# Routing one-hots from bf16 operands, expert owners on GpSimd, an early spare gather, and a new order for the low parts, in a Perceiver block on one core

## What is computed

```python
x = x + xattn(layernorm(x), ctx_1024, ...)   # 4 x 4096 keys of width 256, one head, then w2 on [x, output]
x = x + local_attn(layernorm(x), ...)        # 16 heads, window 64
x = x + moe(layernorm(x), gate_w, wg, wu, wd)
# moe, on 1024 rows of 256, 8 experts of inner width 1024:
logits = x_flat @ gate_w.T
top_v, top_i = top_k(logits, 2); probs = softmax(top_v)
out = sum over experts e of combine[e] * ((silu(x_flat @ wg[e].T) * (x_flat @ wu[e].T)) @ wd[e].T)
```

## Time and profile before

| | |
|---|---|
| median of three runs | 635.04 us (634.96 to 638.15) |
| the profiled execution's own time | 635.36 us |
| its span | 633.6 us |
| mean granted TensorE clock | 0.982 |
| TensorE matmul busy | 598.0 us, 94% of the span |
| VectorE busy | 457.9 us, 72% |
| ScalarE busy | 336.0 us, 53% |
| GpSimd busy | 255.7 us, 40% |
| DMA | 152.62 MB, mean 241 GB/s |

### The profile page before, as it was taken

How to read it: one execution, slowest core, us unless ns; L and a number is a source line. 1 busy time by engine, 2 the same in 40 slices (tenths; PEclk the granted TensorE clock), 3 DMA queues, 4 the chain that set the end, 5 groups by cost and what they waited for, 6 DMA issues and landing times. The chain is left out here.

```text
span 633.6 us, 10820 instructions
## 1 busy us (share of the span) xinstructions
PE 598.0 (94%) x4008; PEld 514.0 (81%) x4008; DVE 457.9 (72%) x803; ACT 336.0 (53%) x603; POOL 255.7 (40%) x313
## 2 busy tenths in 40 slices
PE   8999999899999999999999858999999999999993
PEld 7889988898889988996667646788888888888882
DVE  4867588767886697769888957776767767677750
ACT  4447522762367334554776652656565655657540
POOL 3317820784058433684454613123132332323312
PEclk9999999999999999999999977999999999999998
DMA  8988887899869647861000346999999999999933
GB/s 286 321 305 234 259 324 207 224 278 315 279 190 281 196 134 183 235 172 43 1 3 1 135 141 233 377 333 336 350 323 360 325 343 339 340 353 335 358 100 83
DMA packets 66035, 152.62 MB, mean 241 GB/s; under 512 B 7504, under 2 KB 47952, under 8 KB 55088
## 3 DMA queue, kind: packets, MB, share of 16 engines
q1 hardware_dynamic: 61568, 145.91, 68.8%
q0 software_dynamic: 4416, 6.03, 5.5%
HBM read 121.52 MB, written 31.46 MB: 241 GB/s over the span
## 5 line engine op out<-in xcount | busy, mean ns | idle before, releaser
L630 ACT ACTIVATE wide_high<-region_a 128x1024 fp32r<-128x1024 f32 (+1 forms) x108 | 105.6, 994 | 101.5 <-PE psum L1599 89.6
L1078 DVE TENSOR_TENSOR wide_low<-region_a,wide_high 128x1024 fp32r<-128x1024 f32 x92 | 112.2, 1221 | 64.0 <-ACT wide_high L630 64.0
L566 POOL TENSOR_TENSOR wide_low<-region_a,wide_high 128x512 fp32r<-128x512 f32 x64 | 82.4, 1290 | 18.4 <-ACT wide_high L630 14.4
L1616 PE MATMUL psum<-region_a,region_w 128*128 128x256 f32 x368 | 83.2, 379 | 0.3 <-ACT region_w L630 0.3
L1379 PE MATMUL psum<-turned_high,wide_low 128*128 128x256 f32 x256 | 79.6, 311 | 2.4 <-DVE turned_low L989 1.5
L1599 PE MATMUL psum<-wide_high,turned_low 128*128 128x512 f32 x184 | 77.9, 424 | 1.5 <-issue 0.8
L1616 PEld LDWEIGHTS psum<-region_a,region_w 128*128 128x128 f32 x368 | 69.6, 190 | 10.7 <-issue 0.5
L1379 PE MATMUL psum<-turned_high,wide_high 128*128 128x256 f32 x256 | 72.4, 283 | 0.0
L1379 PE MATMUL psum<-turned_low,wide_high 128*128 128x256 f32 x256 | 72.2, 282 | 0.0
L1599 PE MATMUL psum<-wide_high,turned_high 128*128 128x512 f32 x184 | 72.1, 392 | 0.0
L1599 PE MATMUL psum<-wide_low,turned_high 128*128 128x512 f32 x184 | 71.9, 391 | 0.0
(11 more groups left out here) (201 smaller groups left out, 1205.4 us busy)
## 6 DMA issues: line engine op xcount, KB each, us to landing
region_a<-turned_up SPq DMA_DIRECT2D x23, 2048.0 KB, 9.9
region_a<-turned_down SPq DMA_DIRECT2D x23, 1024.0 KB, 7.5
region_a<-ctx_dram SPq DMA_DIRECT2D x16, 1024.0 KB, 8.9
turned_up<-region_w SPq DMA_DIRECT2D x64, 256.0 KB, 4.2
region_w<-L_ffn_wg_dram SPq DMA_DIRECT2D x16, 512.0 KB, 6.4
region_w<-L_ffn_wu_dram SPq DMA_DIRECT2D x16, 512.0 KB, 6.1
region_w<-L_ffn_wd_dram SPq DMA_DIRECT2D x16, 512.0 KB, 5.8
turned_down<-region_w SPq DMA_DIRECT2D x32, 256.0 KB, 4.2
```

What stands on the lines that cost most here:

```text
L566: nc.gpsimd.tensor_tensor(val_lo[:, g % 4], ctx_sb[n][:, g * PAIR:(g + 1) * PAIR, :], val_hi[:, g % 4].bitcast(F32), ALU.subtract).then_in ...
L630: return nc.scalar.activation(dst, src, ACT.Copy)
L1078: nc.vector.tensor_tensor(w_lo[:, k % RING], group_of(k), w_hi[:, k % RING].bitcast(F32), ALU.subtract).then_inc(low_ready, 1)
L1616: last = nc.tensor.matmul(bank[6][:, 0:D], hidT[n][:, ic * P:(ic + 1) * P], rows, start=ic == 0, stop=ic == IC - 1)
```

## The change

- **Layout and types.** `place_row`, `place_tile`, `place_prob`, `is_tile`, `ways` have the pick as the innermost index now, and `is_tile`, `ways` and the two columns compared (`row_b`, `tile_b`) are bf16. The one-hots compare with full bf16 tables `each_row` and `each_tile` in place of short rows that were broadcast. TensorE reads one pick of them, so with a step of 16 elements (32 bytes).
- **Tables.** GpSimd writes the two tables by `iota` (2048 and 368 columns) into the end of `region_w`, behind its last layer norm work. `row_numbers` and `tileno` go.
- **`tile_i`** (a shift) goes; `tile_b` is slot minus row, so 128 times the tile, and waits for `row_i`.
- **Owners.** `begun` and `owner` leave VectorE. GpSimd computes them on one partition, in seven instructions, each waiting for the one before.
- **Spare gather.** Once the rows and the zeros are stored, GpSimd gathers 128 spare rows into `xg[3]`, ahead of `owners()`; the gathers of the tiles wait for it, and for the tokens.
- **Order of parts.** In each group `xgT_hi*w_lo`, `xgT_hi*w_hi`, then `xgT_lo*w_hi`. Group 0 waits for the high part of the rows, and only its third matmul for the low part.
- **Tile 1's rows.** At j = 0 VectorE splits tile 1's rows ahead of `low(4)` rather than behind it.

```diff
-        place_row = place_row_f.bitcast(BF16).rearrange("p (i r) -> p i r", i=PICKS)
+        place_row = place_row_f.bitcast(BF16).rearrange("p (r i) -> p r i", i=PICKS)
...
+        _, each_tile_f, each_row_f = cut(region_w, [4 * MAT - PICKS * (SLOT_TILES + P) // 2, PICKS * SLOT_TILES // 2, PICKS * P // 2])
...
-        place_tile = place_tile_f.bitcast(BF16).rearrange("p (i v j) -> p i v j", i=PICKS, v=2)
+        place_tile = place_tile_f.bitcast(BF16).rearrange("p (v j i) -> p v j i", i=PICKS, v=2)
...
+            pool.wait_ge(w_stored[1], 16 * QUADS * E * NMAT // 2 + FIRST)
+            nc.gpsimd.iota(each_row, pattern=[[1, P], [0, PICKS]], base=0, channel_multiplier=0,
+                           allow_small_or_imprecise_dtypes=True).then_inc(tables_ready, 1)
+            nc.gpsimd.iota(each_tile, pattern=[[P, SLOT_TILES], [0, PICKS]], base=0, channel_multiplier=0,
+                           allow_small_or_imprecise_dtypes=True).then_inc(tables_ready, 1)
+
+            def owners():
+                pool.wait_ge(first_found, 1)
+                nc.gpsimd.tensor_tensor(begun, tile_start[0:1, :].rearrange("p (a j) -> p a j", a=1).broadcast_to([1, E - 1, SLOT_TILES]),
+                                        first[0:1, 1:E].rearrange("p (e a) -> p e a", a=1).broadcast_to([1, E - 1, SLOT_TILES]),
+                                        ALU.subtract).then_inc(owner_step, 1)
+                pool.wait_ge(owner_step, 1)
+                nc.gpsimd.tensor_scalar(begun, begun, 1.0 / P, 1.0, ALU.mult, ALU.add).then_inc(owner_step, 1)
+                pool.wait_ge(owner_step, 2)
+                nc.gpsimd.tensor_scalar(begun, begun, 0.0, 1.0, ALU.max, ALU.min).then_inc(owner_step, 1)
+                pool.wait_ge(owner_step, 3)
+                nc.gpsimd.tensor_tensor(begun[:, 0:3], begun[:, 0:3], begun[:, 3:6], ALU.add).then_inc(owner_step, 1)
...
+                nc.gpsimd.tensor_copy(owner[0:1, :], begun[:, 0]).then_inc(owner_ready, 1)
...
             pool.wait_ge(rows_stored, 16 * DUOS)
             pool.wait_ge(zero_stored, 16)
+            pool.wait_ge(w_turned, E * NMAT * STEPS)
+            pool.indirect_dma_start(out=xg[AHEAD - 1], out_offset=None, in_=x3_dram,
+                                    in_offset=bass.IndirectOffsetOnAxis(ap=spare_i[:, 0:1], axis=0)).then_inc(spare_gathered, 16)
+            owners()
+            pool.wait_ge(spare_gathered, 16)
             pool.wait_ge(tokens_ready, 1)
...
-            then(nc.vector.tensor_reduce(first[:, :], started, axis=X_AXIS, op=ALU.add))
-            then(nc.vector.tensor_tensor(begun, tile_start[:, :].rearrange("p (j a) -> p j a", a=1).broadcast_to([P, SLOT_TILES, E - 1]),
-                                         first[:, 1:E].rearrange("p (a e) -> p a e", a=1).broadcast_to([P, SLOT_TILES, E - 1]), ALU.is_ge))
-            with nc.allow_low_precision(reason="a count up to 7"):
-                nc.vector.tensor_reduce(owner[:, :], begun, axis=X_AXIS, op=ALU.add).then_inc(owner_ready, 1)
+            nc.vector.tensor_reduce(first[:, :], started, axis=X_AXIS, op=ALU.add).then_inc(first_found, 1)
+            dve.wait_ge(first_found, 1)
...
-            nc.vector.tensor_scalar(row_i[:, :], slot[:, :], P - 1, None, ALU.bitwise_and)
-            then(nc.vector.tensor_scalar(tile_i[:, :], slot[:, :], P.bit_length() - 1, None, ALU.logical_shift_right))
+            then(nc.vector.tensor_scalar(row_i[:, :], slot[:, :], P - 1, None, ALU.bitwise_and))
+            nc.vector.tensor_tensor(tile_b[:, :], slot[:, :], row_i[:, :], ALU.subtract)
+            nc.vector.tensor_copy(row_b[:, :], row_i[:, :])
+            then(nc.vector.tensor_tensor(ways[:, 0, :], way_base[:, :], row_i[:, :], ALU.subtract))
...
+            dve.wait_ge(tables_ready, 2)
+            then(nc.vector.tensor_tensor(is_tile, each_tile, per_pick(tile_b[:, :], SLOT_TILES), ALU.is_equal))
             for v in range(2):
-                nc.vector.tensor_tensor(place_tile[:, :, v, :], is_tile, ways[:, :, v:v + 1].broadcast_to([P, PICKS, SLOT_TILES]), ALU.mult)
+                nc.vector.tensor_tensor(place_tile[:, v], is_tile, per_pick(ways[:, v], SLOT_TILES), ALU.mult)
             for n in range(TOPK):
                 half = slice(n * TILES, (n + 1) * TILES)
-                nc.vector.tensor_tensor(place_row[:, half, :], row_numbers[:, :].rearrange("p (a r) -> p a r", a=1).broadcast_to([P, TILES, P]),
-                                        per_pick(row_i[:, half], P), ALU.is_equal).then_inc(places_ready, 1)
+                nc.vector.tensor_tensor(place_row[:, :, half], each_row[:, :, half], per_pick(row_b[:, half], P), ALU.is_equal).then_inc(places_ready, 1)
...
-                last = nc.vector.tensor_tensor(place_prob[:, :, v, :], is_tile, per_pick(prob_parts[:, v], SLOT_TILES), ALU.mult)
+                last = nc.vector.tensor_tensor(place_prob[:, v], is_tile, per_pick(prob_parts[:, v], SLOT_TILES), ALU.mult)
...
-                if j + 1 < SLOT_TILES:
+                if j == 0:
+                    tile_xgT(1, 1)
+                    low(4)
+                elif j + 1 < SLOT_TILES:
                     low(4 * j + 4)
                     tile_xgT(j + 1, 1 - n)
...
-                    last = nc.tensor.matmul(bank[6][:, 0:2 * SLOT_TILES], place_row[:, i, :], place_tile[:, i].rearrange("p v j -> p (v j)"),
+                    last = nc.tensor.matmul(bank[6][:, 0:2 * SLOT_TILES], place_row[:, :, i], place_tile.rearrange("p v j i -> p (v j) i")[:, :, i],
                                             start=i == 0, stop=i == PICKS - 1)
...
-                        pe.wait_ge(xgT_ready, j + 1)
+                        pe.wait_ge(xgT_high, j + 1)
...
-                        parts = ((xgT_lo, w_hi), (xgT_hi, w_lo), (xgT_hi, w_hi))
+                        parts = ((xgT_hi, w_lo), (xgT_hi, w_hi), (xgT_lo, w_hi))
                         for m, (rows, w) in enumerate(parts):
+                            if g == 0 and c == 0 and m == 2:
+                                pe.wait_ge(xgT_ready, j + 1)
```

39 lines of the change are left out of this document (21 added, 18 removed).

## The result

| | before | after |
|---|---|---|
| runs on the same chip, median | 635.4 us (7 runs) | 639.57 us (7 runs, 638.87 to 641.29) |
| ratio, 95% interval | | 1.0065 [1.005, 1.008] |
| profiled execution | 635.36 us | 639.5 us |
| its span | 633.6 us | 637.8 us |
| mean granted clock | 0.982 | 0.978 |

The change makes the kernel 4.1 us slower. The forecast was 632.9 us, with nothing slower than 636.3 in its range. The two spans differ by 4.2 us, so the pair of profiles can be read for it.

The account below looks back on a forecast made before the run. TensorE bounds the expert loop, and VectorE's routing chain, then TensorE's own order, time its start. Terms -2.03 + 0.75 - 0.45 - 0.45 = -2.18 us took 635.36 to 633.2, forecast as a 632.9 median; range 631.0 to 636.3.

Parts of the forecast that it names:

- Owners on GpSimd: In the routing, GpSimd's seven owner instructions take 4.0 us; tile 1's load goes out later but still in time for ScalarE.
- cover of gather 0: Ahead of tile 0's transposes: gather 0 takes 3.3 to 4.9 us and stays hidden, at worst 0.4 us showing.
- The tables go where GpSimd idles: Before the tokens: GpSimd writes the tables (2416 columns) in its 17.69 us of idle time; no cost was counted.
- Rival 4: TensorE's chain in the routing: the clock comes back sooner, change -3.6 us, time 631.4; chance 0.14.
- rival 2: In the routing, GpSimd's seven owner instructions stretch beside VectorE's work, leaving a gain of 0.8 us, 634.2; chance 0.14.
- Stepped reads: TensorE's inverse and weights matmuls read with a 32-byte step: +0.75 us, between free and a bound of 1.5.
- Rival 1: TensorE's stepped pairs cost more than a load's own length; at 0.16 us a pair other gains are eaten; chance 0.12.
- One-hots from bf16: VectorE's one-hot comparisons in the routing run at twice the rate with 2-byte operands: -1.63 us.
- Owners leave VectorE, and one more wait: VectorE's routing chain: two owner instructions gone, -0.60 us; one added wait for `row_i`, +0.20.
- Spare gather: On GpSimd ahead of gather 0: may shorten the 0.92 us between tokens and gather 0; credited 0.
- Low part last: Start of tile 0: its matmuls begin when the rows' high part is done, not the low part, -0.45 us.
- Tile 1's rows sooner: Start of tile 1: rows split ahead of `low(4)` let it start sooner, net -0.45 us.

Follow-up runs that it names:

- e9: Kernel before, with only the owners moved to GpSimd: ratio 1.0068, 638.17 us.
- e1: Changed kernel, with the two tables written earlier, during local attention (the large one in four pieces): ratio 1.001, 636.97 us.
- e2: Changed kernel, with the owners back on VectorE and the tables still late: ratio 0.9996, 635.62 us.
- e6: e1, with tile 1's load issued only once gather 0 has landed: ratio 1.0043.
- e15: The same kernel as e1, run again in more rounds: ratio 1.0023, 638.06 us.
- e10: Changed kernel, with two more filling matmuls ahead of tile 0's transposes: ratio 1.0031, 637.47 us.
- e4: Kernel before, with the 2048-column table written by GpSimd in the changed kernel's place and never read: ratio 0.9992, 635.08 us.
- e13: e8, with three filling matmuls ahead of the weights instead of four and none behind: ratio 0.9971, 633.96 us.
- e12: e8, with the weights' 16 matmuls moved behind tile 0's up matmuls: ratio 0.9985, 633.2 us.
- e7: e1, without the spare gather: ratio 1.0016.
- e5: Kernel before, with only the loop order changed (low part last, tile 1's rows ahead of low(4)): ratio 0.9991, 635.58 us.
- e8: Changed kernel, with both tables early and owners back on VectorE: ratio 0.998, 635.61 us.
- e11: e8, with the weights' 16 matmuls reading neighbouring columns instead of every 16th: ratio 0.9979, 633.66 us.
- e3: Kernel before, with one-hots stored pick-innermost but still computed from f32 and int32: ratio 1.0186.
- e14: e9, with five filling matmuls instead of one ahead of tile 0's transposes: ratio 1.0039, 637.61 us.
- e16: e8, with two filling matmuls ahead of the weights instead of four and none behind: ratio 0.9979, 634.66 us.

## Why the prediction was wrong

**Owners on GpSimd: the step that failed is the cover of gather 0, "at worst 0.4 shows".** The owners' length was right: 3.57 us, forecast 4.0. That the load would go out later was right, and that the gather would be issued into it was in the text. What was mis-sized is what that does to the gather. I put it at 3.3 to 4.9 us, the upper end from gather 2, which flew beside SyncE's store, so that at worst 0.4 us would show; 1.22 showed in the kernel after and 3.04 in e9. The gather measured 5.9 (after), 6.0 (e1) and 6.3 (e9), and in each of the three it lands within 0.4 us of the load: 391.4 and 391.5, 390.4 and 390.6, 389.5 and 389.9. Where the load landed ahead of it (e2: 387.8 and 388.1) or was issued behind it (e6), the gather took 2.8. The 0.5 us between that and the 3.3 of the kernel before is GpSimd's own instruction, 0.95 us in e2 and 1.49 before: the landing is 1.8 to 1.9 us behind its end in both. The row that I took as the bound had shown as much already. The view of DMA issues, before, has for the store, issued at 388.19:

```profile
sums_by_token<-residual SPq DMA_DIRECT2D x1, 1024.0 KB, 4.8
```

It landed at 393.0, and gather 2, issued at 388.42, at 393.3. I carried over the length of that gather, and not that it lands with the transfer ahead of it; by my own figures the load was to land at 389.7, 2.3 us behind the transposes' 387.4. I had asked only whether the load comes in time for ScalarE.

**The idle TensorE costs a second time, and no step had that.** Rival 4 asked whether the clock would come back sooner; it did, in the window from 387.50, in place of 388.5. The same row showed nothing of what a pause behind it does. In the kernel after it fell 0.8 us into a pause of 1.2, and tile 0's first matmuls ran at about 0.43 us apart: this ate the 0.8 us that tile 1 gained (+0.03 in the table). In e1's profile a pause of 1.75 us left the clock up; in that of e15, the same kernel, it fell in a pause of 1.25. So it is a chance that a pause brings, and the filled versions price it at 1 to 2 us. Nor is the sooner return shown to be the change's: e10 has the same instructions up to the fillers behind the weights, and its clock came back at 392.25.

**"The tables go where GpSimd idles": right for GpSimd, wrong for VectorE.** GpSimd did idle there, but VectorE ran the norm beside it, and its instruction became 2.35 us long. It ended 0.14 us behind the second table (369.32 + 0.54), in e4 0.15 behind the first. The Trainium skill (SBUF — State Buffer, "Who interferes with whom") says that VectorE's `tensor_scalar` in a two-port mode and GpSimd block each other for a whole instruction; these two rows agree, the second table's 0.54 us included. I had applied the rule to the owners (rival 2) and not to the tables. What it costs is less settled. Alone nothing (e4, 0.9992). Undone in the changed kernel, e15 gives 0.4% back and e1 0.5%. One part of the first maximum's lateness is the clock: it fell at 370.5 in the kernel after, ahead of the last 16 logits matmuls, and at 371.5 before, in the middle of them; they took 3.42 us for 2.32. This fall moves by itself: from the norm to the first maximum the four profiles with a late table show 5.5 to 6.9 us and all others 3.5 to 6.5, and e4's has 5.53 without a loss in its time. A cost of 0.2% would fit both e4's interval and the difference between the kernel after and e15; whether the table costs more in company than alone stays open.

**Stepped reads: right direction, too small.** From the end of `place_row` to the end of the inverse it is 1.12 us, before 0.55 (+0.57); the weights +1.16. That is 1.7, forecast 0.75, bound 1.5. The bound was "each pair takes as long as its weight load, 0.117". The inverse stayed inside its part of it (0.79), the weights went beyond theirs (0.73). The 0.117 was read from the inverse alone; the weights' matmuls had longer loads already in the kernel before. Views of line 1562 before and of line 1582, the inverse, after (shortest, median, longest ns):

```profile
L1562 PEld LDWEIGHTS psum<-region_s x16: 133/138/151, 386.4 to 387.6; 128*128 128x128 bf16 x16
```

```profile
L1582 PEld LDWEIGHTS psum<-region_s x16: 142/149/170, 382.5 to 383.8; 128*128 128x128 bf16 x16
```

Nor does a pair follow its load: in the kernel after, the loads of inverse and weights are equally long (median 0.149 and 0.148), but a pair of the inverse, with 46 moving columns, takes 0.104 us and one of the weights, with 69, 0.144. That points to the moving operand, at an estimated 0.040 / 23 = 1.7 ns a column from these two figures; no run varied it alone. Rival 1 asked for this, and its break-even, 0.16 us a pair, was not reached. The note on 16-byte lines in the Trainium skill (SBUF — State Buffer, "Door 1: The DMA port swizzle") agrees in direction: a step of 32 bytes goes to a new line each time. The doubling that I weighed is what 1.14 (before) and 2.29 (e13) show at 1.2 GHz; at 2.4 GHz it is threefold, 0.71 (e9) to 2.31 (e12).

**One-hots from bf16: right.** -1.50, forecast -1.63. A `place_row` takes 0.702 us; before, the two took 2.35. The view of line 1178, shortest, median and longest ns:

```profile
L1178 DVE TENSOR_TENSOR region_s<-region_w,row_of_pick x2: 682/702/722, 381.7 to 382.3; 128x1024 bf16<-128x1024 bf16 x2
```

The Trainium skill (VectorE: DVE Perf Modes, "The perf-mode tier table") has twice the rate for this, and for the part of the time that goes by columns the trace now agrees.

**Owners leave VectorE, and one more wait: -0.17, forecast -0.40.** From `first_tile` to `is_tile` it is 2.02 us, before 2.19. Beside GpSimd's steps VectorE's own became slower, `row_i` 0.28 for 0.17 and the two of `picked` 0.47 for 0.36; in e2, without those steps, they are back at 0.17 and 0.36. That is rival 2's contention, with the other engine paying.

**Spare gather: 0, as forecast.** No gain can be seen in e7 either.

**Low part last: right.** In e2, at full clock, transposes to first matmul are 0.46 us shorter, forecast 0.45.

**Tile 1's rows sooner: right to tile 1, wrong to the end.** Tile 1 gained 0.8 in e5, forecast 0.45. But it does not come off the end. Tile 2's up load is issued only when a buffer of tile 0's is read, and ScalarE waits for it 2.24 us in the kernel after and 2.29 in e5, 1.25 before. Over both tiles e5 gains nothing (-0.80 + 1.02). "Each microsecond by which the loop starts earlier should come off the end" does hold, as far as tile 2, for the start of tile 0: from its first matmul to tile 2's first silu it is 19.9 to 20.1 us in e1, e2, e5, e8, e10 and e11, whose tile 0 starts 16.1 to 18.9 us behind the first maximum (before: 17.44, and 19.82 from there). e2 and e8 come out only even because they start tile 0 only 1.04 and 0.67 us sooner, not the 2 us and more of the forecast, and lose 0.2 of it by tile 2 (0.84 and 0.46).

**Later in the loop,** the +0.81 us is one late load at tile 13. The profiles of e3, e6, e10, e12, e14 and e15 have 0.3 to 0.9 us there too, those of e11, e13 and e16 at other tiles, and those of the kernel before, e1, e2, e4, e5, e7, e8 and e9 at most 0.25 at any. As e1 and e15 are the same kernel and e3 and e14 have little of the change in them, it moves from execution to execution and is not the change's.

**In sum.** The forecast's -2.18 and the span's +4.2 are 6.4 us apart. By the stretches of the first table: 1.85 lie ahead of the routing's first maximum, where I had nothing; 0.6 up to the tokens (-1.12, forecast about -1.7), half of it the stepped reads of the inverse; 1.9 up to tile 0's first matmul (+1.88, forecast about 0), of which 0.8 lies ahead of the wait (some 0.7 of it the weights' stepped reads, by e11), 1.2 is the wait for gather 0, and behind it 0.15 is gained, the low part's 0.46 less 0.3 for the lowered clock; 0.5 at tile 1 (the gain eaten by the lowered clock); 1.0 at tile 2's load; 0.8 at tile 13; and -0.2 at the end. These were read from one pair of profiles, whose stretches move by a microsecond or two from run to run. What the ratios show is shorter: with the owners on VectorE the loss is gone (e2), and with the owners on GpSimd alone it is all there (e9). One slip of the prediction changes nothing: its upper end, 636.3, is a rival 1 with pairs of 0.20 us; 0.21 would give 636.6.

## What to carry to other kernels

When a step is moved to a slower engine, follow what it releases to the end: here the result was not late for anyone, but the load that it released now flew together with a gather that the critical chain needs, and the gather landed when the load did. Take from a row when a transfer landed beside another, not only how long it took. Work put where its own engine idles can still hold up a neighbour, as the tables did VectorE. And a pause of TensorE just behind the return of its clock may have to be paid twice: take it away, or else fill it.

## What the runs showed that I had not expected

- A gather issued 1.5 to 2 us behind a 2 MB load lands with the load (5.9 to 6.3 us), and in 2.8 us when the load lands ahead of that (e2) or is issued later (e6).
- TensorE's pairs of 69 columns that read both operands with a step of 32 bytes take 0.144 us at 1.2 and at 2.4 GHz; plain ones take 0.071 and 0.044. Pairs of 46 columns take 0.104 with the step and 0.061 without, at 1.2 GHz.
- VectorE writing 2-byte results with a step of 32 bytes took 4.6 us for 1024 columns (e3), and 1.2 with neighbours side by side (before).
- GpSimd's writing of its tables, which reads nothing from memory, held a 0.41 us norm instruction of VectorE until it was done: 2.35 us with both tables (after), 1.85 with the large one alone (e4).
